# A state-space layer and a mixture of experts on one core: the first stage written anew, its successor's first tables loaded ahead, and the splitting of the shared weights moved into the recurrence

## The reference, cut to what matters

```
# layer 1, xn = layernorm(x)
xp = xn @ W_x                      # 512 -> 64 + 16 + 16
dt = softplus(xp[:, :64] @ W_dt + b_dt)
B, C = xp[:, 64:80], xp[:, 80:96]
h = exp(dt * A) * h + (dt * xn) * B     # token by token, 16 states per channel
y = sum over states of h * C + xn * D_skip
x1 = x + layernorm(y)
# layer 2, xt = layernorm(x1)
out = top-2 of 8 experts (512 -> 2048 -> 512, capacity 640) of xt
    + 0.2 * (gelu(xt @ sw1 + sb1) @ sw2 + sb2 + gelu(xt @ swd) @ swu)   # the shared expert
result = x1 + layernorm(out)
```

## Time and profile before

| | us |
|---|---|
| three timed runs: median (lowest to highest) | 3754.85 (3750.47 to 3764.85) |
| the profiled execution: time | 3755.44 |
| its span, first to last instruction | 3753.7 |
| busy: PE, DVE, POOL, ACT | 3126.7, 1910.4, 1692.5, 1391.4 |
| last transfer of `prepare` issued | 262.20 |
| first instructions of `mix` | 267.96 |
| first scan of the recurrence | 330.29 |

### The profile page before, as it was taken

The page is one execution under the profiler, slowest core; times in us unless marked ns, Lnnn a source line. Parts: engine busy times, 40 slices in busy tenths (PEclk is TensorE's granted clock), DMA queues, the critical chain, the costliest instruction groups (busy, mean ns, idle before and its releaser), DMA issues. The chain is left out here.

```text
span 3753.7 us, 45229 instructions
## 1 busy us (share of the span) xinstructions
PE 3126.7 (83%) x15062; PEld 2561.3 (68%) x15062; DVE 1910.4 (51%) x2835; ACT 1391.4 (37%) x2451; POOL 1692.5 (45%) x1458
## 2 busy tenths in 40 slices
PE   3322568898899899699999999999999999999960
PEld 1101347677777777578888888888888888888850
DVE  6744998999989996164222222222222322223228
ACT  4532457667676675221131221312213122122114
POOL 4653668798887896441050330502305114041025
PEclk8665569999999999798999999999999999999985
DMA  6764639779679685650130220302203112031039
GB/s 192 259 213 89 137 101 239 203 204 264 193 221 245 198 242 171 185 182 29 37 102 20 76 71 22 113 23 65 74 14 105 45 56 85 15 97 52 14 116 343
DMA packets 282074, 480.15 MB, mean 128 GB/s; under 512 B 30896, under 2 KB 106496, under 8 KB 281872
## 3 DMA queue, kind: packets, MB, share of 16 engines
q1 hardware_dynamic: 222976, 296.62, 26.8%
q0 software_dynamic: 56704, 180.38, 16.2%
q10 hardware_dynamic: 2192, 0.36, 0.1%
HBM read 380.18 MB, written 97.11 MB: 127 GB/s over the span
## 5 line engine op out<-in xcount | busy, mean ns | idle before, releaser
L1375 DVE CAST hh<-h 128x512 fp32r<-128x512 f32 (+1 forms) x400 | 157.7, 394 | 1301.5 <-ACT h L1227 1301.3
L788 POOL TENSOR_TENSOR u<-dtxs,Bt 128x512 f32<-128x512 f32 x512 | 663.1, 1313 | 254.5 <-DVE b_psA L697 219.2
L1227 ACT ACTIVATE h<-c_psH,b1e 128x512 f32<-128x512 f32 (+1 forms) x384 | 237.3, 618 | 1355.1 <-PE c_psH L1546 1312.9
L697 DVE TENSOR_TENSOR_SCAN b_psA<-b_psA,carry,u 128x512 f32<-128x512 f32 x512 | 656.8, 1283 | 42.4 <-ACT b_psA L587 42.1
L882 PE MATMUL b_psY<-ident,pr 128*128 128x128 f32 x2048 | 350.8, 310 | 282.6 <-DVE pr L704 261.4
L1295 POOL DMA_INDIRECT xrow<-xt_d,idx x80 | 90.4, 1130 | 1097.4 <-PE c_psT L1537 602.3
L1588 PE MATMUL c_psY<-W2h,hh 128*128 128x512 f32 x1344 | 535.1, 398 | 1.9 <-DVE hl L1377 1.8
L1588 PE MATMUL c_psY<-W2h,hl 128*128 128x512 f32 x1344 | 526.4, 392 | 0.0
L1588 PE MATMUL c_psY<-W2l,hh 128*128 128x512 f32 x1344 | 526.3, 392 | 0.0
L882 PEld LDWEIGHTS b_psY<-ident,pr 128*128 128x128 f32 x2048 | 268.1, 158 | 370.9 <-DVE pr L704 313.5
L704 DVE TENSOR_TENSOR pr<-b_psA,Ct 128x512 f32<-128x512 f32 x512 | 354.3, 692 | 17.7
(11 more groups left out here) (250 smaller groups left out, 5691.1 us busy)
## 6 DMA issues: line engine op xcount, KB each, us to landing
w<-ws_d POOLq DMA_DIRECT2D x224, 512.0 KB, 6.4
raw<-in_w SPq DMA_DIRECT2D x256, 256.0 KB, 2.8
Bt<-bc_d SPq DMA_DIRECT2D x64, 512.0 KB, 16.2
Ct<-bc_d SPq DMA_DIRECT2D x64, 512.0 KB, 19.8
y_d<-yst SPq DMA_DIRECT2D x80, 256.0 KB, 2.0
xin<-in_x SPq DMA_DIRECT2D x8, 1024.0 KB, 10.5
wr<-in_sw SPq DMA_DIRECT2D x32, 256.0 KB, 4.1
ws_d<-wh SPq DMA_DIRECT2D x8, 1024.0 KB, 7.1
```

What stands on the lines that cost most here:

```text
L697: nc.vector.tensor_tensor_scan(psA[q][:, :], psA[q][:, :], u[g % U_RING][:, :], carry[:, k:k + 1], ALU.mult, ALU.add).then_inc(s_h, 1)
L788: nc.gpsimd.tensor_tensor(u[g % U_RING][:, :], dtx[s % 2][:, :], Bt[n // TG][:, n % TG, :], ALU.mult)\
L1227: nc.scalar.activation(h32[:, 0:n * P], psH[j % 2][:, 0:n * P], ACT.Gelu, bias=b1[:, j - 1:j]).then_inc(s_gelu, 1)
```

## The change

`prepare` is written anew, in single chunks with lags of 0 to 3 steps. The bias enters as one more row of `wdt` against a row of ones in `xpT`, so that no engine adds it. GpSimd has only the four small operations of the normalization's factors; ScalarE copies `xnT` out of `psT`, and takes Abs straight from `psZ`; VectorE makes `w1` = 1 + u, `low` = (w1 - 1) - u, then max(z, 0) + ln out of `psZ`, less `low`, and times `xnT`. There is one set of `u`, `w1`, `low`, `lg` instead of two, `psZ` is held until VectorE has read it, and `xn` and `xnT` have three buffers. The product with `D_skip` goes: `xT_d` holds the turned normalized rows, and TensorE multiplies them by a diagonal matrix `Dg` in `mix`, in a full product instead of a turning one.

At step 5 SP issues the 16 tables of chunk 0 and the first passes' dt and dtx, whose tiles now live across the barrier. The splitting of the shared weights is in `mix`: 16 pieces of twice 128 rows, one every 6 units from unit 2 (ScalarE) and 5 (VectorE) on, the last at 92 and 95; SP stores the rounded half at 6i + 4 and the rest at 6i + 6, with a raw load behind it. The small weights' split is at units 6 and 10. The first shared weights are read back at units 84 (`w1`) and 110 (`w2`) instead of 32 and 36.

```diff
+            def load_first_scans():
+                sp.wait_ge(s_obc[0], 16)
+                for j in range(NG):
+                    load_table(sp, bc_d, early["Bt"], early["s_B"], 0, j, 0)
+                    load_table(sp, bc_d, early["Ct"], early["s_C"], NS, j, 0)
...
+            for i in steps(2, 4):
+                if 0 <= i + 2 < NCH:
+                    load(i + 2)
+                if 0 <= i - 1 < NCH:
+                    store_xT(i - 1)
+                if 0 <= i - 2 < NCH:
+                    store_bc(i - 2)
+                if 0 <= i - 3 < NCH:
+                    store_dt(i - 3)
+                if i == 5:
+                    load_first_scans()
...
+            def project(c):
                 act.wait_ge(s_xp, c + 1)
                 after(act, s_z, c - 1)
+                after(act, s_obc[c % 2], c // 2 * 16)
+                nc.scalar.copy(xpT[c % 2][0:NX, :], psX[0:NX, :]).then_inc(s_xpT, 1)
...
+            for i in steps(0, 3):
+                if 0 <= i - 1 < NCH:
+                    evacuate(i - 1)
+                if 0 <= i < NCH:
+                    norm(i)
+                if 0 <= i - 2 < NCH:
+                    decay(i - 2)
+                if 0 <= i - 1 < NCH:
+                    project(i - 1)
+                if 0 <= i - 2 < NCH:
+                    log(i - 2)
...
+            def finish(c):
+                q = c % 2
+                dve.wait_ge(s_lg, c + 1)
+                after(dve, s_odt[q], c // 2 * 16)
+                v.scalar_tensor_tensor(dt[q][:, :, :], psZ[:, :, :], 0.0, lg[:, :, :], ALU.max, ALU.add).then_inc(s_r, 1)
+                dve.wait_ge(s_r, c + 1)
+                dve.wait_ge(s_low, c + 1)
+                v.tensor_tensor(dt[q][:, :, :], dt[q][:, :, :], low[:, :, :], ALU.subtract).then_inc(s_dt, 1)
+                dve.wait_ge(s_dt, c + 1)
+                dve.wait_ge(s_xnT, (c + 1) * DT)
+                after(dve, s_odx[q], c // 2 * 16)
+                v.tensor_tensor(dx[q][:, :, :], dt[q][:, :, :], xnT[c % XR][:, :, :], ALU.mult).then_inc(s_dx, 1)
...
+            def step_size(c):
+                pe.wait_ge(s_xpT, c + 1)
+                after(pe, s_r, c)
...
+SPLIT = 6
...
+            def split_hi(i):
+                act.wait_ge(s_wr[i % 4], (i // 4 + 1) * 32)
+                after(act, s_whs[i % 2], i // 2 * 16)
+                after(act, s_wl, i - 1)
+                nc.scalar.copy(halves(hh, i), raw_pair(i)).then_inc(s_wh, 1)
...
+            def split_lo(i):
+                dve.wait_ge(s_wh, i + 1)
+                after(dve, s_wls[i % 2], i // 2 * 16)
+                nc.vector.tensor_tensor(halves(hl, i), raw_pair(i), halves(hh, i).bitcast(F32), ALU.subtract)\
+                    .then_inc(s_wl, 1)
...
+                if g % SPLIT == 5 and g // SPLIT < FC:
+                    split_lo(g // SPLIT)
...
-                    last = nc.tensor.matmul(psY[:, t, :], sk[:, t * P:(t + 1) * P], ident[:, :],
-                                            start=False, stop=True, is_transpose=True, skip_group_check=True)
+                    last = nc.tensor.matmul(psY[:, t, :], sk[:, t * P:(t + 1) * P], Dg[:, s % DT, :],
+                                            start=False, stop=True, skip_group_check=True)
```

More of the change, by code:

```diff
@@ L52, in pass_gate, with prepare @@
     eng.sem_inc(gate, 1)
[L55 to L89, removed]
+def prepare(nc, sem, const, early, x, A_log, D_skip, W_x, W_dt, b_dt, dt_d, dtx_d, bc_d, xT_d):
+    ident, A_neg, eps, Dg = const["ident"], const["A_neg"], const["eps"], const["Dg"]
     NX = RANK + 2 * NS
+    XR = 3
     with ExitStack() as ctx:
@@ L133, in prepare, with steps @@
+        s_oxT = [sem(f"a_xT_stored{q}") for q in range(XR)]
         block = ctx.enter_context(nc.Block("prepare"))
+        def steps(lead, lag):
+            return range(-lead, NCH + lag)
         @block.sync
         def _(sp):
[L137 to L178, removed]
@@ L181, in _ @@
+            for c in range(NCH - XR, NCH):
+                sp.wait_ge(s_oxT[c % XR], (c // XR + 1) * 16)
         @block.gpsimd
@@ L220, in _, with evacuate @@
-            act.wait_ge(s_w, 64)
-            def norm(i, q):
-                c = i * 2 + q
-                act.wait_ge(s_mv, (c + 1) * CT)
-                nc.scalar.activation(sd[q][:, :], mv[q][:, :, 1], ACT.Sqrt, bias=eps[:, :]).then_inc(s_sd, 1)
+            def evacuate(c):
+                after(act, s_dx, c - XR + 1)
+                after(act, s_oxT[c % XR], c // XR * 16)
+                for d in range(DT):
+                    act.wait_ge(s_xT, c * DT + d + 1)
+                    nc.scalar.copy(xnT[c % XR][:, d, :], psT[d % 2][:, :]).then_inc(s_xnT, 1)
@@ new lines, in one_plus @@
+            def one_plus(c):
+                dve.wait_ge(s_u, c + 1)
+                after(dve, s_lg, c)
+                v.tensor_scalar(w1[:, :, :], u[:, :, :], 1.0, None, ALU.add).then_inc(s_w1, 1)
+                dve.wait_ge(s_w1, c + 1)
+                after(dve, s_dt, c)
+                v.scalar_tensor_tensor(low[:, :, :], w1[:, :, :], -1.0, u[:, :, :], ALU.add, ALU.subtract)\
+                    .then_inc(s_low, 1)
+            v.memset(wdt[RANK:NX, :], 0.0).then_inc(s_pad, 1)
+            for q in range(2):
+                v.memset(xpT[q][NX:NX + 1, :], 1.0).then_inc(s_pad, 1)
@@ new lines, in load_raw @@
+            def load_raw(i):
+                after(sp, s_wl, i - 3)
+                for o in range(2):
+                    if i < FC // 2:
+                        f = (2 * i + o) * P
+                        sp.dma_start(raw_pair(i)[:, o, :].rearrange("p (a f) -> p a f", a=DT),
+                                     w["sw1"].rearrange("(a p) f -> p a f", p=P)[:, :, f:f + P]).then_inc(s_wr[i % 4], 16)
+                    else:
+                        r = (2 * i + o - FC) * P
+                        sp.dma_start(raw_pair(i)[:, o, :], w["sw2"][r:r + P, :]).then_inc(s_wr[i % 4], 16)
```

454 lines of the change are left out of this document (239 added, 215 removed).

## The result

The changed kernel took 3665.16 us in the median of four runs (3659.25 to 3668.89), the kernel before 3759.85 beside it (3750.47 to 3766.76): a ratio of 0.9748, 95% interval 0.972 to 0.9777. It is faster by some 95 us; 3666 was forecast, from 3755.4 for the kernel before. The profiled execution spans 3667.1 us, before 3753.7: 86.6 less. It is the slowest of the changed kernel's four runs, so times read from the two profiles give a smaller gain than the medians.

The account below looks back on a forecast made before the run. Stage one was bounded by a loop of waits, the first scan by small weights queued behind tables, chunk 0 by VectorE. From 3755.4: -131 + 29.3 + 2 + 5 + 5 = -89.7, giving 3666 us; 8-in-10 range 3615 to 3715.

Parts of the forecast that it names:

- The start: Stage one up to z(0): the old path through load, statistics, factors and norm, with z(0) ready at about 36 us.
- The loop: Stage one from z to z: one `psZ` and one set of softplus tiles close a loop, taken as 15.5 us.
- The rival of a half clock: Stage one: TensorE stays at half clock, z product 7.2 us, loop 20.6 us, total 3691 us; chance 0.16.
- The stall: Stage one: ScalarE's projection copy of chunk 6 waits for a store behind the tables, 31 us, bounds 12 and 36.
- The recurrence: Chunks 0 and 1: 16 VectorE pieces of 1.83 us, 29.3, plus 2 for small weights, cost 31; 41 lost in all.
- The 5 us for late tables: Around units 45 to 70: tables, pieces and passes share SP's queue, late tables hold the scan; 5 us, bounds 0 and 15.
- the 5 for the skip products: Skip products in `mix` become full 32-bit ones; 13 of 28 passes at 0.4 us each, 5 us, at most 14.
- ScalarE's rounding: Recurrence: 16 pieces of 0.95 us cost nothing in chunk 0; if the cover fails, 0.2 us a piece, 3 us.
- no later chunk would be longer by more than 1 us: Sign of being wrong: one of chunks 2 to 7 longer than before by more than 1 us.
- The blocking of VectorE by GpSimd: Recurrence: with two SBUF operands each, VectorE stands until GpSimd is through; 0.69 + 1.14 = 1.83 us a piece.
- The rule on table loads: Stage one: the skill adds a 1.38 us drain per table change, loop 18 us; the prediction left it out.
- Slower or the same: Two rivals: queue below 126 GB/s over the first 96 units, chance 0.03; stage one held until about 290, chance 0.04.

Follow-up runs that it names:

- experiment 2: The changed kernel without its early loads, tables and first passes loaded at the start of `mix` again; 3665.82 us, ratio 0.9745.
- experiment 3: The changed kernel with four `xpT` buffers instead of two, and four semaphores for their stores; 3665.13 us.
- experiment 7: The changed kernel with the skip added by turning products against the identity again, `D_skip` left out of the result; 3657.01 us, ratio 0.9733.
- experiment 6: The changed kernel with each of VectorE's pieces issued between the scan and the product of its unit; 3654.14 us, ratio 0.9731.
- experiment 1: The kernel before with the small weights issued ahead of dt, skip and the 16 tables at the start of `mix`; 3731.78 us, ratio 0.9918.

## Why the prediction was right

*Stage one.* Sizes were off and cancelled, which was luck. The start was 7 us too late (36 instead of 29.2 for z(0)): I had taken the old path over, which began behind the load of `A_log`, and overlooked that the changed kernel's doesn't. The loop was put at 15.5 us; the reads of `psZ` lie 15.8, 18.1, 15.9 and 18.2 apart (36.76, 52.55, 70.67, 86.58, 104.75), 17.0 in the mean, because from the second on the z product took 4.5 to 6.9 us instead of 3.7. From 54 to 62 us, in such a product, the granted clock was 0.54, near the 1.2 GHz level. Before it TensorE had stood idle for the copies out of `psT`, some 5 us; but the same 5.05 us stand before z products of 4.60 us (at 73.11) and of 6.88 (at 89.02), so what decides between the two is not shown (in experiment 2's kernel the same products took 5.7 us each, and the reads of `psZ` lay 17.0 apart from the first on):

```profile
54.00:62.00 8.00, 8.00 (x14) 3.58 (x13) 7.83 (x8) 4.15 (x7) 0.00 (x0) 0.54 0.64 206
...
54.99 6.82 PE L302 MATMUL a_psZ<-xpT,wdt 97*128 97x512 f32 x8
...
71.17 1.97 PE L294 MATMUL a_psT<-ident,xn 128*128 128x128 f32 x8 [5.05 <-ACT xnT L194]
```

The rival of a half clock had the right size for single products (6.9 of 7.2). The projection behind each took 3.60 us (from 61.9 to 65.2 us the granted clock was 1.00), not the 6.9 that the rival needs, so that no step reached its 20.6 us. On the way to 197.4: the burst was issued at 78 instead of 83 and the store of B and C of chunk 4 had landed by 145.9 instead of 150; from there to `mix` it was 51.5 us instead of 47, with z products of 6.02 and 5.90 us.

*The stall.* 31 us were worked out, 28.9 came, at the place and by the store that was named; experiments 2 and 3 show that it is the tables' transfer and not the buffer. The mechanism was right. What the prediction failed to draw from its own numbers is that the gain from loading ahead was gone by it: it priced the stall (31) and never the alternative (tables in `mix`, small weights out of their way), which experiment 2 measures as equal.

*The recurrence.* 10 pieces of 1.83 and 2.0 for the small weights are 20.3 in chunk 0 (measured 20.0), 6 pieces are 11.0 in chunk 1 (11.9). The 5 us for late tables did not come (chunk 1 had 0.9 in all beyond its pieces), the 5 for the skip products came out as 8 by experiment 7's times and as 9.1 in the chunks; these two misses cancelled by luck, and the sum of 41 was met by 41.0. ScalarE's rounding cost nothing in chunk 0, as assumed: from 199 to 346 us VectorE waited for no exp. The sentence that no later chunk would be longer by more than 1 us contradicted the 5 us charged to them; all six are longer, by 0.8 to 2.4. The blocking of VectorE by GpSimd was read from two rows that don't belong together: the operation of 4.50 us in the earlier trace rows ran at 203.43. The one under way at 229.72 was this:

```profile
227.68 6.47 POOL L202 TENSOR_TENSOR au<-au,w 128x2048 f32<-128x2048 f32 x1 [1.62 <-DVE w L314]
```

It ended at 234.15, and the piece 2.15 us later, at 236.30, so the reading holds. Its own 6.47 us are 1.97 more than 4.50, which is about what VectorE's line 315 (227.51 to 229.80, two operands in SBUF) had left to run when it was issued: the wait goes both ways.

*The rule on table loads* (the Trainium skill, "ScalarE: Activation LUTs", "What ACT_TABLE_LOAD costs"), which adds a drain of 1.38 us: after Abs ends at 160.11 the load begins at 160.13, lasts 1.28, and Exp begins at 161.42 in the changed kernel. The trace shows no drain beyond it, here as before.

*Slower or the same* needed the queue below 126 GB/s, or stage one to last to 290; it carried 173 and 199 GB/s over chunks 0 and 1 and 250 where it was fullest.

## What to carry to other kernels

A transfer queue is a line of its own: what is issued ahead of need stands in front of what is needed now, and small loads that everything waits for belong ahead of large ones. Before crediting a prefetch, price the same transfers started late but in the right order, since the consumer may use them as they land. When an engine's operation is moved out of the way, look at how full the queue is at the next burst; here some 29 us were taken off VectorE, the transfers ahead were at 92%, and 12 us arrived. A single profile can't settle a difference of 1% inside a stage: the same six chunks of the same instructions took 875.5 and 885.3 us.

## What the runs showed of the hardware

A VectorE subtraction with two operands in SBUF waited for a GpSimd operation with two such operands to finish, and then ran at full rate (1208 ns alone, 1793 behind the rest of a u, 2343 at most), while products with one operand in PSUM stayed at 692 ns beside the same GpSimd operations; the Trainium skill says the same ("SBUF — State Buffer", section "Terms": the port pair is held for the full instruction, and the loser blocks), and experiment 6 turns it round by starting VectorE first. SP's issuing of transfers is itself held when much is under way: the 16 tables took from 78.05 to 116.96 us to issue, where the first of the earlier trace rows took 0.43 us, and in the kernel before `sb2` took 16.20 us behind the tables and 1.11 in experiment 1 ahead of them. And a full 32-bit product of 128 columns is two instructions of 275 ns where a turning product is one of 273.
